# The inputs of the second attention's queries are turned by VectorE in 32x32 blocks and by way of memory, in place of TensorE's transposes

## What is computed

```python
x = x + tanh(g_xattn[0]) * L0_xattn(layernorm(x), ctx, mask, ...)   # 32 heads, most of the time
x = x + tanh(g_ffn[0])   * L0_ffn(layernorm(x), 4-bit weights, ...)  # x @ W + bias
x = x + tanh(g_xattn[1]) * L1_xattn(layernorm(x), ctx, ...)
x = x + tanh(g_ffn[1])   * L1_ffn(layernorm(x), ...)                 # base product and adapters

def L1_xattn(text, features, ...):          # one head, 512 wide
    fn = rmsnorm(features) * fn_w
    Q = rmsnorm(text @ Wq.T + bq) * qn_w    # text is the tile that the change is about
    K = rmsnorm(fn @ Wk.T + bk) * kn_w
    return softmax(Q @ K.T / sqrt(512)) @ fn
```

## Time and profile before

| | |
|---|---|
| runs, median | 951.73 us (950.13 to 952.33) |
| profiled execution | 950.68 us |
| its span, first to last instruction | 948.9 us |
| busy: TensorE / VectorE / GpSimd / ScalarE | 99% / 62% / 52% / 42% |
| granted TensorE clock, mean | 1.000 |
| query loop, first to last query product starts | 856.22 to 889.30 us |

### The profile page before, as it was taken

How to read it: one execution, slowest core, us unless ns; L and a number is a source line. 1 busy time by engine, 2 the same in 40 slices (tenths; PEclk the granted TensorE clock), 3 DMA queues, 4 the chain that set the end, 5 groups by cost and what they waited for, 6 DMA issues and landing times.

```text
span 948.9 us, 15361 instructions
## 1 busy us (share of the span) xinstructions
PE 936.7 (99%) x4818; PEld 792.2 (83%) x4818; DVE 592.7 (62%) x1021; ACT 403.2 (42%) x1088; POOL 495.4 (52%) x463
## 2 busy tenths in 40 slices
PE   9999999999999999999999999999999999999998
PEld 8888777888888888888888888888888888888886
DVE  4788845485538554765476546664576967756754
ACT  4765424343344333433334334433442336657730
POOL 3847554464536463746374636563556335698630
PEclk9999999999999999999999999999999999999999
DMA  8146486775767676776677666867686655232002
GB/s 286 46 140 229 158 304 255 265 272 220 265 245 276 243 265 226 271 266 249 237 253 273 258 244 221 298 241 253 236 285 255 240 207 190 122 104 97 1 1 89
DMA packets 71556, 203.64 MB, mean 215 GB/s; under 512 B 10208, under 2 KB 25056, under 8 KB 70496
## 3 DMA queue, kind: packets, MB, share of 16 engines
q1 hardware_dynamic: 70512, 201.87, 58.9%
q10 hardware_dynamic: 1008, 1.32, 0.5%
HBM read 176.95 MB, written 26.21 MB: 214 GB/s over the span
## 4 chain that ended last, share of the span: by engine, by line
PE 89%; POOL 3%; DVE 3%; DMA 2%; ACT 2%; issue 1%; SPq 0%; DVEq 0%; POOLq 0%; ACTq 0%
PE bank L1974 27%; PE bank L1990 18%; PE bank L2051 17%; PE bank L2155 7%; PE bank L2007 6%; PE bank L2023 5%; PE bank L1950 3%; PE bank L2179 1%; DMA stage<-in_w 1%; DMA ring<-combined 1%; PE bank L2035 1%; PE bank L2236 1%; PE bank L2257 1%; PE bank L2300 1%; POOL acc L839 1%
## 5 line engine op out<-in xcount | busy, mean ns | idle before, releaser
L2051 PE MATMUL bank<-wvo,ao 128*128 128x512 f32 x768 | 180.1, 391 | 0.9 <-issue 0.6
L1990 PE MATMUL bank<-wvo,ct 128*128 128x512 f32 x768 | 177.7, 390 | 0.0
L2051 PEld LDWEIGHTS bank<-wvo,ao 128*128 128x128 f32 x768 | 142.8, 188 | 30.5 <-issue 1.6
L1990 PEld LDWEIGHTS bank<-wvo,ct 128*128 128x128 f32 x768 | 143.5, 188 | 29.4
L637 POOL TENSOR_TENSOR wvo<-stage,wvo 128x512 fp32r<-128x512 f32 x64 | 84.9, 1350 | 155.7 <-ACT wvo L940 155.7
L1974 PE MATMUL bank<-ring,wkq 128*128 128x512 f32 x648 | 158.8, 392 | 3.7 <-DMA ring<-combined 2.3
L1974 PEld LDWEIGHTS bank<-ring,wkq 128*128 128x128 f32 x648 | 120.6, 188 | 29.3 <-DMA ring<-combined 2.8
L1461 DVE SCALAR_TENSOR_TENSOR acc<-bank,gated_rows,acc 128x512 f32<-128x512 f32 x128 | 93.1, 742 | 39.3 <-PE bank L2051 38.3
L986 ACT ACTIVATE bank<-bank,nmax 128x128 f32<-128x128 f32 x256 | 88.2, 351 | 64.2 <-DVE nmax L1423 64.2
L1452 DVE TENSOR_TENSOR ao<-bank,ao 128x512 fp32r<-128x512 f32 x64 | 43.9, 691 | 97.5 <-ACT ao L992 97.5
L1483 DVE TENSOR_TENSOR qt<-bank,qt 128x512 f32<-128x512 f32 x98 | 66.3, 690 | 61.4 <-PE bank L1974 53.8
(11 more groups left out here) (187 smaller groups left out, 1533.4 us busy)
## 6 DMA issues: line engine op xcount, KB each, us to landing
ring<-combined SPq DMA_DIRECT2D x216, 512.0 KB, 6.5
stage<-in_w SPq DMA_DIRECT2D x63, 512.0 KB, 4.2
passing<-turned_blocks SPq DMA_DIRECT2D x24, 512.0 KB, 2.9
keyed<-passing SPq DMA_DIRECT2D x96, 128.0 KB, 3.0
combined<-work SPq DMA_DIRECT2D x16, 512.0 KB, 4.2
xraw<-in_x SPq DMA_DIRECT2D x2, 1024.0 KB, 11.6
bias<-in_bias SPq DMA_DIRECT2D x8, 256.0 KB, 4.6
cs<-in_ctx SPq DMA_DIRECT2D x1, 2048.0 KB, 7.8
```

The costliest lines, as they stand in the source:

```text
L1990: mm = pe.matmul(bank[un_of[m][u] % RING][:, :], ct[:, i, c, b * P:(b + 1) * P], wvo[:, j, c, :], start=(c == 0 and i + j == 0), stop=(c = ...
L2051: mm = pe.matmul(bank[to][:, :], ao[:, h, p, b * P:(b + 1) * P], wvo[:, j, 2 * pair + h, :], start=(h == 0 and p + j == 0), stop=(h == 1 a ...
```

## The change

The tile of the queries (n = 1) is no longer turned by TensorE. VectorE turns it in 32x32 blocks in its place in `xnr` (`tile_turned`), SP writes it to the memory tensor `passing_tiles` (`tile_passed`) and fetches it back into the same place in four transfers of 32 partitions (`tile_back`). `hi` and `lo` of n = 1 read `xnr` instead of a bank. After this trip, partition 32j + k and chunk c hold input column 128j + 32c + k, so the query weights are loaded in that order, in four transfers instead of one. `xnr` keeps four tiles as before, but the slots for n = 0 and n = 1 are told apart (`normed_slot`), and `normed(u, 1)` runs earlier in the lists of ScalarE. `T(u, 1)` is gone from TensorE's list. On GpSimd `key_root(7)` goes ahead of `norm(5, 1)`.

```diff
+    passing_tiles = nc.dram_tensor("passing_tiles", (B, 4, 32, 4, KC * 32), fp32, kind="Internal").ap()
...
-        slot = lambda u, n: (u % 2, 2 + u % 2, u % HB)[n]
+        slot = lambda u, n: (u % 2, (u + 2) % HB, u % HB)[n]
+        normed_slot = lambda u, n: (u % 2, (u + 2) % HB, (u + 2) % HB)[n]
...
-                sp.dma_start(raw_k[:, :, :], a["w_qry"]).then_inc(s_raw["qry"], 16)
+                for j in range(4):
+                    sp.dma_start(raw_k[32 * j:32 * j + 32, :, :], a["w_qry"][:, j, :].rearrange("(c k) n -> k c n", c=KC)).then_inc(s_raw["qry"], 16)
...
+                def tile_passed(u):
+                    sp.wait_ge(S["T1"], u + 1)
+                    sp.dma_start(passing_tiles[u, :, :, :, :].rearrange("i k j c -> (i k) j c"),
+                                 xnr[:, normed_slot(u, 1), :].rearrange("p (j c) -> p j c", j=4)).then_inc(s_tpassed[u % 2], 16)
+                def tile_back(u):
+                    sp.wait_ge(s_tpassed[u % 2], TPASSED[u % 2] + 16 * (u // 2) + 16)
+                    for j in range(4):
+                        sp.dma_start(xnr[32 * j:32 * j + 32, normed_slot(u, 1), :].rearrange("k (i c) -> k i c", i=4),
+                                     passing_tiles[u, :, :, j, :].rearrange("i k c -> k i c")).then_inc(s_tback[u % 2], 16)
...
+                keys_passed(2)
+                tile_passed(2)
+                keys_back(2)
+                tile_passed(3)
+                tile_back(2)
+                keys_passed(3)
+                tile_passed(4)
+                tile_back(3)
+                keys_back(3)
+                for u in range(5, B):
+                    tile_passed(u)
+                    tile_back(u - 1)
+                tile_back(7)
...
                 def hi(u, n):
+                    if n == 1:
+                        act.wait_ge(s_tback[u % 2], TBACK[u % 2] + 64 * (u // 2) + 64)
+                        if u >= 4:
+                            act.wait_ge(S["q_mm"], u - 3)
+                        elif u >= 2:
+                            act.wait_ge(S["y0"], 5 + u)
+                        act.activation(tt[:, slot(u, 1), 0, :, :].rearrange("p c (i t) -> p i c t", i=4),
+                                       xnr[:, normed_slot(u, 1), :].rearrange("p (i c t) -> p i c t", i=4, c=KC),
+                                       ACT.Copy).then_inc(S["hi1"], 1)
+                        return
...
-                    if u in (4, 5, 7):
-                        normed((u - 4) if u < 6 else 2, 1)
+                    if u in (2, 3):
+                        normed(u - 2, 1)
+                    elif u >= 5:
+                        normed(u - 3, 1)
...
-                    if u < 5:
-                        normed(u + 3, 1)
+                    if u < 3:
+                        normed(u + 5, 1)
...
+                def tile_turned(u):
+                    dve.wait_ge(S["xn1"], u + 1)
+                    blocks = xnr[:, normed_slot(u, 1), :].rearrange("p (f k) -> p f k", k=32)
+                    dve.transpose(blocks, blocks).then_inc(S["T1"], 1)
...
+                    if u in (3, 4):
+                        tile_turned(u - 3)
+                    elif u >= 6:
+                        tile_turned(u - 4)
...
+                    if u < 4:
+                        tile_turned(u + 4)
...
                     if u < 6:
                         T(u + 2, 0)
-                    else:
-                        T(u - 6, 1)
...
                     queries(u)
-                    if u < 6:
-                        T(u + 2, 1)
```

More of the change, by code:

```diff
@@ L327, in build @@
         s_kpassed, s_kback = s_mneg, s_k0
+        s_tpassed, s_tback = (s_passed, s_bias), (s_keyed, s_place[1])
+        TPASSED, TBACK = (16 * GROUPS * TURNED, 16 * GROUPS), (64 * GROUPS * TURNED, 16 * (4 * (GROUPS - 2) + 2 + 1))
         half = lambda s: slice(s * 512, s * 512 + 512)
@@ L602, in _, with keys_passed @@
                 sp.wait_ge(s_o, last_out)
-                for pair in range(HB):
+                def keys_passed(pair):
                     sp.wait_ge(S["k_T"], 2 * pair + 2)
@@ L606, in _, with keys_back @@
                                  kraw[:, pair % 3, :, :, :, :].rearrange("p j c u k -> p j (c u k)")).then_inc(s_kpassed, 16)
-                    if pair == 1:
-                        sp.wait_ge(s_tlo["qry"], KC)
-                        sp.dma_start(raw_k[:, 0:2, :].rearrange("p a (b n) -> p (a b) n", b=2), a["w_ra"]).then_inc(s_raw["ra"], 16)
+                def keys_back(pair):
                     sp.wait_ge(s_kpassed, 16 * pair + 17)
@@ L613, in _ @@
                                      passing_keys[pair, :, :, j, :].rearrange("i k c -> k i c")).then_inc(s_kback, 16)
+                def tile_passed(u):
[7 more added lines that the diff above has]
+                                     passing_tiles[u, :, :, j, :].rearrange("i k c -> k i c")).then_inc(s_tback[u % 2], 16)
+                keys_passed(0)
+                keys_back(0)
+                tile_passed(0)
+                keys_passed(1)
+                tile_passed(1)
+                tile_back(0)
+                sp.wait_ge(s_tlo["qry"], KC)
+                sp.dma_start(raw_k[:, 0:2, :].rearrange("p a (b n) -> p (a b) n", b=2), a["w_ra"]).then_inc(s_raw["ra"], 16)
+                keys_back(1)
+                tile_back(1)
+                keys_passed(2)
[11 more added lines that the diff above has]
+                tile_back(7)
                 for u in range(B):
@@ L859, in _ @@
                         key_root(u + 2)
+                    if u == 6:
+                        key_root(7)
                     if u:
                         norm(u - 1, 1)
-                    if u == 6:
-                        key_root(7)
                     if u < 4:
@@ L1024, in split_hi @@
                     raw, hi, lo = wchunk(n, c)
-                    act.wait_ge(s_raw[n], 64)
+                    act.wait_ge(s_raw[n], 112 if n == "qry" else 64)
                     if n in ("key", "ffn"):
@@ L1179, in normed @@
                     act.wait_ge(S[f"nr{n}"], u + 1)
-                    if n == 2 and u < 2:
-                        act.wait_ge(S["T0"], 7 + u)
+                    if n == 0 and u >= 2:
+                        act.wait_ge(S["T0"], u - 1)
+                    elif n == 1 and u >= 4:
+                        act.wait_ge(S["lo1"], u - 3)
+                    elif n == 1 and u >= 2:
+                        act.wait_ge(S["T0"], 5 + u)
                     elif n == 2 and u < 4:
-                        act.wait_ge(S["T1"], 5 + u)
+                        act.wait_ge(S["lo1"], 5 + u)
                     elif n == 2:
                         act.wait_ge(S["T2"], u - 3)
-                    elif u >= 2:
-                        act.wait_ge(S[f"T{n}"], u - 1)
-                    dst, src = xnr[:, slot(u, n), :], acc[:, u, :]
+                    dst, src = xnr[:, normed_slot(u, n), :], acc[:, u, :]
                     if n == 0:
@@ L1574, in lo @@
                     dve.wait_ge(S[f"hi{n}"], u + 1)
+                    if n == 1:
+                        blocks = lambda t: t.rearrange("p c (i t) -> p i c t", i=4)
+                        dve.tensor_tensor(blocks(tt[:, slot(u, 1), 1, :, :]),
+                                          xnr[:, normed_slot(u, 1), :].rearrange("p (i c t) -> p i c t", i=4, c=KC),
+                                          blocks(tt[:, slot(u, 1), 0, :, :]).bitcast(fp32), ALU.subtract).then_inc(S["lo1"], 1)
+                        return
                     dve.tensor_tensor(tt[:, slot(u, n), 1, :, :], bank[4 + u % 2][:, :].rearrange("p (c t) -> p c t", c=KC),
@@ L2187, in T @@
                     elif n:
-                        pe.wait_ge(S[f"lo{n - 1}"], 7 + u)
+                        pe.wait_ge(S["lo0"], 7 + u)
                     else:
                         pe.wait_ge(s_dev, x1_done(4 + u))
-                    turned(4 + u % 2, xnr[:, slot(u, n), :], f"T{n}")
+                    turned(4 + u % 2, xnr[:, normed_slot(u, n), :], f"T{n}")
                 def tile_product(u, n, b, w, width, done, last=True):
```

## The result

| | before | changed |
|---|---|---|
| runs, median of 6 | 952.43 us (950.13 to 952.92) | 966.12 us (964.13 to 967.45) |
| profiled execution / span | 950.68 / 948.9 us | 967.33 / 965.5 us |
| busy TensorE / VectorE | 99% / 62% | 97% / 62% |
| first to last query product | 33.08 us | 46.39 us |

The ratio is 1.0146, 95% interval 1.0128 to 1.0163: slower by 1.5%, 13.7 us between the medians, against 11.9 forecast (963.6 us; the range was 956.5 to 969.5).

The account below looks back on a forecast made before the run. TensorE, hardly pausing in the query stage, was taken as the bound. Added waits of 16.3 less 3.5 (transposes) and 0.9 (two waits) gave +11.9 us: 951.73 + 11.9 = 963.6 us, range 956.5 to 969.5.

Parts of the forecast that it names:

- The loop: Query stage queues: lo, turn two tiles later, passing, return of the tile between, hi, lo; 6.4 us against TensorE's 5.07 round.
- Where the loss falls: TensorE's query stage: 4.7 us standing for the copy of query 0 before query 1, 3.1 us at tile 2.
- the rival of the half pace: TensorE after pauses: matmuls at half pace, 3 us more, +14.9, 966.6 us; chance 0.17 shared with choked SP issues.
- All pauses together: TensorE's added waits, from a product before the query stage through the query rounds, summed to 16.3 us.
- The landing: Tile return from memory, issue to landing of 64 KB transfers: taken as 2.6 us, ends 1.8 and 3.7.
- the prediction's own walk: Query stage, each start the latest of its waits plus the row's duration: +11.9 us, last query product at 901.2.
- tile 2's return: SP's queue, behind the key return and tile 3's passing: issued 861.3 to 862.7, landed 865.3.
- The turns on VectorE, the weights in four pieces, the moved steps: Eight turns (5.5 us of VectorE) cost only where they stand in the loop; four-piece weight load and moved steps cost nothing.
- hi 0.65 and lo 0.69 from SBUF: ScalarE's hi and VectorE's lo reading SBUF: 0.65 and 0.69 us, ranges 0.58 to 0.80 and 0.6 to 0.75.
- Hidden after all: Rival: the trip is shorter than TensorE's rounds, so the kernel gets 4.4 us faster, 947.3 us; chance 0.07.

Follow-up runs that it names:

- e1: Changed kernel with VectorE's list reordered: key turn and turn of tile u+4 ahead of query(u) and lo(u+2); 956.1 us, ratio 1.0039 to the kernel before.
- e7: Changed kernel with only SP's list of passages, returns and last weight load reordered; 960.26 us, ratio 1.0089 to the kernel before.
- e2: Changed kernel without the trip through memory: VectorE turns the blocks and hi reads the tile as it stands; 949.89 us, ratio 0.997 to the kernel before.
- e3: Changed kernel with ScalarE's hi(u+2) moved behind query_out(u-1) and query_squares(u); 965.82 us, ratio 1.0142 to the kernel before.
- e11: e9 with tile 4's return issued right behind its passage, ahead of the last key pair's and tile 5's passages; 950.11 us, ratio 0.9991 to the kernel before.
- e6: Changed kernel with e7's SP list, e1's VectorE edit, and tiles 2 and 3 turned one round earlier; 954.95 us, ratio 1.0033 to the kernel before.
- e10: Changed kernel with one weight load on SP moved behind tile 1's return; 967.2 us, ratio 1.0161 to the kernel before.
- e9: Changed kernel with tiles 0-3 turned by TensorE, 4-7 turned one round earlier, last key return behind returns of tiles 4 and 5; 952.27 us, ratio 1.0004.

## Why the prediction was right, and where it was off

- *The loop, not the length of the trip, sets the loss.* Shown. e1 takes 10 us back with every operation and transfer in place, e7 5.4 by SP's list alone, e2 all of it by leaving the trip out, and e3 shows that moving ScalarE's wait gains nothing. Forecast 6.4 us a turn, measured 6.68 in the mean. That closeness is partly luck: the turns took 7.24, 7.58, 5.82, 6.99 and 5.77 us, so one with nothing in its way takes 5.8, less than forecast, and slips make up the rest. The chain has the steps that I named, in that order.
- *Where the loss falls.* I forecast the longest pause, 4.7 us, at the transposes of query 1, and 3.1 at the product of tile 2. Measured: 1.90 and 3.19, and between them the product that took 2.5 us longer. 3.1 + 4.7 = 7.8 forecast and 3.19 + 2.47 + 1.90 = 7.6 measured: the slow product lay in time that TensorE would have stood anyway, for ScalarE's copy. So the rival of the half pace had the mechanism (the granted clock fell in 868 to 880) and, as far as the trace shows, the wrong price: 3 us forecast for it, nothing to 2.4 found. All pauses together: 12.95 + 2.47 = 15.4 us, forecast 16.3.
- *What a pause costs.* The pauses came out shorter than forecast and the loss larger, because the sum prices a pause at its length alone. Between the first and the last query product has 33.08 - 0.93 of pauses - 6 x 0.44 of transposes = 29.5 us of work; the changed kernel has 46.39 - 15.4 = 31.0. A group ahead of a pause runs to its full length (2.99, 0.63 or 1.13 us) where the next group otherwise starts after 2.77, 0.44 or 0.89, some 0.2 us more for each pause. Seven pauses more than before fit the 1.5 us. By the same count, slow products taken off too, e2, with two pauses as before, has 0.2 us over, and e7, with eight, 1.6.
- *The landing.* Sized 2.6, measured 2.2 in the middle, 1.9 to 4.0. That term was too large. The Trainium skill's estimate of 2.15 us for 64 KB (DMA: Bandwidth & Descriptors, on the anatomy of one DMA) agrees with the middle of 2.2. By the points of the prediction's own walk (+6.9 at 1.8, +9.2 at 2.15, +11.9 at 2.6) a landing of 2.2 gives some +9.5, an estimate and further from the result than +11.9: the forecast was close partly because errors cancelled.
- *The other error.* I had tile 2's return issued from 861.3. It went out from 866.73, 2.1 us later with 3.3 taken off. The key passage ahead of it took 3.9 us where I had 2.6, but that isn't what held it: SP was through with the key return at 865.73 and then stood for the turn of tile 3, which I had as done by 860.9. The chain of waits of 845 to 915 has, ahead of that turn:

```profile
859.36 3.57 DMA xnr<-passing_tiles
862.95 0.64 ACT tt L1252
...
865.65 0.68 DVE xnr L1667
```

That turn stands behind lo of tile 1, and lo behind hi, which waited for tile 1's return. The walk has no landing for that return at all. Its four transfers were issued right behind a weight load and four key returns and took 3.6 to 4.0 us to land. e3 bears this out: there the key passage was usable after 2.9 us, SP still stood for tile 3's turn, until 863.00, and hi of tile 2 came 10.36 us behind the first query product, 10.63 in the changed kernel. Only part of the lateness is the return's: the turn of tile 3 was over 6.8 us behind the first query product, 6.2 in e2, which has no trip, and 5.0 in the forecast. The rest lies in VectorE's own list. With 3.3 us taken off, hi of tiles 2 to 6 comes 1.6, 2.2, 1.5, 2.1 and 1.4 us later than forecast: the offset is there at tile 2 and hardly grows.
- *The slips in the loop.* A lo of 1.37 us at 870.85 in place of 0.69, a landing of 3.13 us for tile 5, four issues in 2.37 us for tile 3. They were not tried one by one.
- *The turns on VectorE, the weights in four pieces, the moved steps: nothing.* Not contradicted: e2 contains them all, is faster than before, and leaves at most 1.5 to 2.0 us to them. The weights took 7.2 us to land and were first read at 820.90, 3.6 us after the earlier trace rows; the first query product of this execution comes 3.3 us later, too.
- *hi 0.65 and lo 0.69 from SBUF.* 0.63 and 0.69.
- *Hidden after all, 947.3 us.* Not in this order of the lists, as I said. With other lists half of the trips are hidden (e11). Whether all eight can be was not settled: e6, the best with all of them, has three pauses over 0.5 us in the query stage (0.85, 1.68 and 1.96) and one product at 4.38 us, and the longest of them hangs on a passage that landed late.

## What to carry to other kernels

When work goes from a busy engine to an idle one and a queue of transfers, price the order of the queues ahead of the length of the trip: draw the loop of who stands behind whom, and compare one turn of it with the busy engine's round. A step that waits for a transfer belongs behind everything on its engine that starts the next transfer; moving two calls took back 10 of 13.7 us here. Give a transfer a lead by turning early, see to it that its return is not queued behind a passage that waits for something later, and ask what else is in the same queue at that moment: e6 lost its longest pause to that.

## What the runs showed of the hardware

- A key passage of 512 KB took 2.6 us where little stood beside it (before), and 2.9 in e3, issued 1.5 us behind the last of a weight load and eight small returns. Issued 0.3 us behind the same it took 3.9 (changed), and 5.05 where the load stood last, right ahead of it (e10). In these runs what was just issued ahead moved the landing by up to 2.4 us at the same size.
- A tile's passage of 256 KB landed in 2.0 us by itself and in 4.4 in e6, 0.6 us behind a key passage in a busy queue.
- The four issues of a tile's return took 1.73 us at the least, and 2.84 for e6's tile 4; no row explains the extra.
- A product of 12 matmuls took 5.46 us at a granted clock of 0.50 and 2.99 at 1.00. But after a pause of 2.01 us in the changed kernel the next product took 2.96 us, while in e9, after pauses of 1.25 and 0.59 us, it took 4.39 (granted clock 0.57 from 876 to 880). The length of the pause alone doesn't tell which.
- VectorE turns 128x512 in blocks in 0.66 to 0.71 us, from and to the same buffer, as long as an elementwise step of that size (0.65 to 0.74).
